# An attention and feed-forward block: turning tiles in 32 by 32 blocks on VectorE, and the mixing in two halves

## What is computed

```
qkv = x @ qkv_w + qkv_b;  16 heads of 16;  local attention over the 128 newest tokens -> local
latent part: 64 pooled tokens, 4 heads; softmax; remote = lat_out @ rout_w + rout_b
gate  = sigmoid(local @ gl_w + remote_h @ gr_w)            # one value per token and head
mixed = gate * local + (1 - gate) * remote_h
x1 = layernorm(x + mixed @ out_w + out_b)
h  = gelu(ternary_linear(x1, w_up));  y = layernorm(x1 + ternary_linear(h, w_down))
```

## Time and profile before

| | |
|---|---|
| median of three runs | 1155.28 us (1149.62 to 1156.93) |
| the profiled execution | 1154.15 us, of which the span of its instructions is 1152.4 us |
| PE busy | 88% of the span |
| DVE / POOL / ACT busy | 78% / 61% / 59% |
| mean granted PE clock | 0.965 |
| one sequence in the steady part | 66 us (first exponentials at 483.05 and 549.12 us) |

### The profile page before, as it was taken

How to read it: one execution, slowest core, us unless ns; L and a number is a source line. 1 busy time by engine, 2 the same in 40 slices (tenths; PEclk the granted TensorE clock), 3 DMA queues, 4 the chain that set the end, 5 groups by cost and what they waited for, 6 DMA issues and landing times.

```text
span 1152.4 us, 37627 instructions
## 1 busy us (share of the span) xinstructions
PE 1019.2 (88%) x15616; PEld 642.4 (56%) x15616; DVE 902.5 (78%) x2119; ACT 682.4 (59%) x1076; POOL 698.0 (61%) x874
## 2 busy tenths in 40 slices
PE   5878999999999999999999999999999999986855
PEld 2445565655556565655656565565656555564533
DVE  6688888887887988787888888788788878875445
ACT  2425666656666665666666565666666566664523
POOL 7216675656667576566757565566756565673744
PEclk9889999999999999999999999999999999996877
DMA  7740604325060423416061331616042250600000
GB/s 219 204 125 14 193 21 120 87 77 148 32 193 23 145 61 104 121 42 182 24 167 56 113 94 59 166 33 187 28 131 77 85 139 33 174 23 20 2 19 18
DMA packets 46662, 108.18 MB, mean 94 GB/s; under 512 B 7542, under 2 KB 26486, under 8 KB 43382
## 3 DMA queue, kind: packets, MB, share of 16 engines
q1 hardware_dynamic: 46348, 105.78, 31.9%
q10 hardware_dynamic: 144, 0.00, 0.0%
HBM read 71.58 MB, written 34.08 MB: 92 GB/s over the span
## 4 chain that ended last, share of the span: by engine, by line
PE 44%; DVE 28%; ACT 16%; issue 5%; POOL 3%; DMA 2%; SPq 1%; DVEq 0%; POOLq 0%; ACTq 0%
PE oacc L1459 8%; PE work L1537 7%; PE oacc L1480 6%; PE work L1398 5%; PE scores L1439 4%; ACT Pt L792 4%; PE work L1469 3%; DVE Pt L974 3%; DVE nmax L1048 3%; DVE x L1111 2%; DVE rem L1115 2%; PE scores L1377 2%; ACT hbuf L828 2%; PE work L1403 2%; DVE oT L1176 2%
## 5 line engine op out<-in xcount | busy, mean ns | idle before, releaser
L792 ACT ACTIVATE Pt<-scores 128x1024 f32<-128x1024 f32 (+1 forms) x256 | 228.6, 915 | 104.5 <-PE oacc L1459 63.8
L1048 DVE TENSOR_REDUCE nmax<-work 128x3 f32<-128x480 f32 x352 | 218.1, 637 | 25.2 <-PE work L1403 20.0
L656 POOL TENSOR_TENSOR h_lo<-hbuf,h_hi 128x512 f16<-128x512 f32 x128 | 148.2, 1158 | 130.7 <-DVE h_hi L1170 130.7
L628 POOL TENSOR_SCALAR_AFFINE_SELECT Pt<-Pt 128x512 f32<-128x512 f32 x256 | 166.8, 652 | 91.2 <-ACT Pt L792 90.0
L615 POOL TENSOR_TENSOR parts<-Pt,parts 128x512 bf16<-128x512 f32 x64 | 72.9, 1157 | 138.2 <-ACT parts L728 138.2
L1459 PE MATMUL oacc<-Pt,Vp 128*32 128x256 f32 (+1 forms) x2048 | 150.2, 360 | 5.8 <-DVE ytok L1192 2.7
L1398 PE MATMUL work<-Ks,Qs 98*32 98x160 bf16 x4096 | 139.8, 235 | 11.4 <-DVE nmax L1048 7.4
L1439 PE MATMUL scores<-Qs,Ks 100*32 100x160 bf16 (+4 forms) x4096 | 114.8, 230 | 23.5 <-ACT Pt L792 15.9
L1480 PE MATMUL oacc<-wdn_t,h_hi 128*128 128x256 f16 x512 | 118.2, 273 | 5.6 <-POOL h_lo L656 5.6
L632 POOL TENSOR_SCALAR_AFFINE_SELECT Pt<-Pt 128x512 f32<-128x512 f32 x192 | 122.0, 635 | 0.0
L1297 PE MATMUL scores<-xT,wqk 128*128 128x512 f32 x256 | 114.9, 602 | 6.1 <-DMA xT<-x_t 6.1
(11 more groups left out here) (158 smaller groups left out, 1952.9 us busy)
## 6 DMA issues: line engine op xcount, KB each, us to landing
parts_scratch<-parts SPq DMA_DIRECT2D x96, 256.0 KB, 4.5
Qs<-parts_scratch SPq DMA_DIRECT2D x96, 256.0 KB, 4.7
Ks<-parts_scratch SPq DMA_DIRECT2D x96, 256.0 KB, 4.9
xT<-x_t SPq DMA_DIRECT2D x16, 512.0 KB, 6.6
xres<-x SPq DMA_DIRECT2D x16, 512.0 KB, 7.2
y<-ytok SPq DMA_DIRECT2D x16, 512.0 KB, 3.4
nat<-up_t SPq DMA_DIRECT2D x1, 1024.0 KB, 9.6
nat<-down_t SPq DMA_DIRECT2D x1, 1024.0 KB, 11.8
```

Of the source, the lines that this page charges most:

```text
L628: ins = pool.affine_select(out=pt[:, :, 0:P], in_=pt[:, :, 0:P], compare_op=ALU.is_gt, fill=0.0, base=0, pattern=[[0, 4], [1, P]], channel ...
L656: pool.tensor_tensor(h_lo[:, t % NR, :], hbuf[:, t % 2, :], h_hi[:, t % NR, :], ALU.subtract).then_inc(h_lo_ready, 1)
L792: nc.scalar.activation(Pt[:, u % NPT, :, 0:w], scores[:, slot, :, :].rearrange("p k (h q) -> p (k h) q", h=2)[:, :, 0:w], ACT.Exp, scale=S ...
L1048: nc.vector.tensor_reduce(nmax[:, :, :].rearrange("p b h -> p (b h)")[:, first:first + n], work[:, slot, 0:n * BAND].rearrange("p (h c) -> ...
```

## The change

The output of a head group is turned by DVE straight from `oacc`, in blocks of 32 by 32 (`nc.vector.transpose`), so that tokens mod 32 lie on the partitions of each quadrant, and heads are spread over the four quadrants. The `O` transposes on PE and ACT's copy to `oT` go. The remote part is made transposed by PE (weights stationary, 256 tokens moving: four products, and a fifth for the gate's column in `REMOTE + 1`), ACT adds the bias into `remT` and `remgT` in five passes of 128x256, and DVE turns them into the same form. The gate's ops work on it; the exponential becomes a tanh. The mixing is done for 256 tokens at a time: two products and a sum of 128x512, and a block transpose straight into `mixT`, which `OUT` of that half reads; `MIX_T`, its transposes and ACT's copies go. The two `OUT` steps move up beside `QK + 3`. The maxima are turned by DVE once per sequence (`split_maxima`, at u = 16) and go into `Qs` by 16 small DMAs with no stop in DRAM; their place in SP's queue is now before the store. The reciprocals after the powers go (power of -0.5). ACT does the four last normalising passes, in `GATE` and at `QK + 2` of the next sequence. `pooled` is made one sequence earlier, after `UP + 6`. Weights' columns are put in the order of the quadrants on the host.

The core of the diff, in the order of the file:

```diff
-    ("F", GATE), ("P", QK), ("P", QK + 1), ("P", QK + 2), ("P", QK + 3), ("F", MIX_T),
-    ("P", LAT_RQ), ("F", OUT), ("P", LAT_RKV), ("F", OUT + 1), ("P", VALUES), ("P", LAT_SCORES), ("F", NORM),
+    ("F", GATE), ("P", QK), ("P", QK + 1), ("P", QK + 2), ("F", OUT), ("P", QK + 3),
+    ("F", OUT + 1), ("P", LAT_RQ), ("P", LAT_RKV), ("P", VALUES), ("P", LAT_SCORES), ("F", NORM),
...
+POOL_AT = ("F", UP + 6)
+NORMALISE_AT = {("F", GATE): (0, 1), ("P", QK + 2): (2, 3)}
...
-                for t in range(2):
-                    slot, k = work_use(s, "T", t)
...
+                wait_alone(sp, nmax_split, count(s, 1, 0))
+                for j in range(2):
+                    row = Qs[s.par][MAXR + j:MAXR + j + 1, :, :].rearrange("a h n -> a (h n)").rearrange(
+                        "a (k r w) -> a k r w", k=2, w=P)
+                    for g in range(NG):
+                        quadrant = slice(g * GT, (g + 1) * GT)
+                        for k in range(2):
+                            sp.dma_start(row[:, k, :, quadrant], nmax_pair[quadrant, j, k * GT:(k + 1) * GT]
+                                         ).then_inc(nmax_in[s.par], 16)
...
             def body(s):
                 later = s.second_next()
-                if later.exists:
-                    load_x(later)
+                if s.third_next().exists:
+                    load_x(s.third_next())
                 load_xres(s)
+                if not s.last:
+                    move_max(s.next())
                 if not s.first:
                     store_before(s)
-                if not s.last:
-                    move_max(s.next())
                 if later.exists:
...
+                if k == REMOTE:
+
+                    if not s.first:
+                        act.wait_ge(rem_turned, count(s, 2, -1))
+                    for i in range(2):
+                        bank, n = p_use(s, R_REM + i)
+                        act.wait_ge(p_full[bank], n + 1)
+                        for t in range(KT):
+                            ins = nc.scalar.activation(remT[:, t, i * HALF:(i + 1) * HALF],
+                                                       p_bank(bank)[:, t * HALF:(t + 1) * HALF], ACT.Identity,
+                                                       bias=brem[:, t:t + 1])
+                        ins.then_inc(p_taken[bank], 1)
...
-            def copy_o(s, hg):
-
...
+            def normalise_before(s, b):
+
+                if b == 0:
+                    act.wait_ge(fin_ready, count(s, 1, -1))
+                nc.scalar.activation(y2[:, b, :], y2[:, b, :], ACT.Identity, scale=fin[:, 0, b:b + 1],
+                                     bias=fin[:, 1, b:b + 1]).then_inc(y_ready, 1)
...
-                    nc.scalar.activation(gate[:, 1, :, :], gate[:, 0, :, :], ACT.Exp, scale=-1.0
+                    nc.scalar.activation(gate[:, 1, :, :, :], gate[:, 0, :, :, :], ACT.Tanh, scale=0.5
                                          ).then_inc(gate_e, 1)
-                if k == MIX_T:
-                    for t in range(KT):
-                        act.wait_ge(mix_T, count(s, KT, t))
-                        nc.scalar.activation(mixT[:, t, :], oacc[:, t, :], ACT.Copy).then_inc(mixT_in, 1)
...
+                if k == REMOTE:
+                    dve.wait_ge(rem_copied, count(s, 2, 0))
+                    for t in range(KT):
+                        ins = nc.vector.transpose(rem[:, s.par, t, :, :].rearrange("p b d -> p (b d)"), remT[:, t, :])
+                    ins.then_inc(rem_turned, 1)
+                if k == REMOTE + 1:
+                    dve.wait_ge(rem_copied, count(s, 2, 1))
+                    nc.vector.transpose(remg[:, s.par, :, :].rearrange("p b d -> p (b d)"), remgT[:, :]
+                                        ).then_inc(rem_turned, 1)
...
+            def split_maxima(s):
+
+                for v in (NM - 2, NM - 1):
+                    slot, k = work_use(s, "A", v)
+                    dve.wait_ge(w_taken[slot], k + 1)
+                if not s.first:
+                    dve.wait_ge(nmax_in[1 - s.par], (s.half + s.par) * 16 * 4 * NG)
+                nc.vector.transpose(nmaxT[:, :], nmax[:, :]).then_inc(nmax_vec, 1)
+                dve.wait_ge(nmax_vec, count(s, 2, 0))
+                nc.vector.tensor_copy(nmax_pair[:, 0, :], nmaxT[:, :]).then_inc(nmax_vec, 1)
+                dve.wait_ge(nmax_vec, count(s, 2, 1))
+                nc.vector.tensor_tensor(nmax_pair[:, 1, :], nmaxT[:, :], nmax_pair[:, 0, :], ALU.subtract
+                                        ).then_inc(nmax_split, 1)
 
             def take_o(s, hg):
 
-                slot, k = work_use(s, "O", hg)
-                dve.wait_ge(w_full[slot], k + 1)
...
+                dve.wait_ge(pv_done, count(s, NU, NB * hg + NB - 1))
+                nc.vector.transpose(o_q[:, hg // 2, :, hg % 2, :],
+                                    oacc[:, hg % 2, :].rearrange("p (b d) -> p b d", d=GT)).then_inc(o_taken, 1)
...
-                    z, e, ng, r, a = (gate[:, j, :, :] for j in range(5))
-                    done(nc.vector.tensor_tensor(e, o_tok[:, :, :, VN], dead[:, :, :], ALU.add))
-                    done(nc.vector.reciprocal(r, e))
-                    done(nc.vector.tensor_tensor(a, o_tok[:, :, :, HD], r, ALU.mult))
-                    nc.vector.tensor_tensor(z, a, rem[:, s.par, :, D:RW], ALU.add).then_inc(gate_z, 1)
+                    dve.wait_ge(o_taken, count(s, HG, HG - 1))
+                    z, e, ng, r, a, half_r = (gate[:, j, :, :, :].rearrange("p t b m -> p (t b m)")
+                                              for j in range(6))
+                    of_heads = o_q[:, :, :, :, :].rearrange("p t b m d -> p (t b m) d")
+                    done(nc.vector.tensor_tensor(a, of_heads[:, :, VN],
+                                                 dead[:, :, :, :].rearrange("p t b m -> p (t b m)"), ALU.add))
+                    done(nc.vector.reciprocal(r, a))
+                    done(nc.vector.tensor_tensor(a, of_heads[:, :, HD], r, ALU.mult))
+                    dve.wait_ge(rem_turned, count(s, 2, 1))
+                    for t in range(KT):
+                        of_t = [gate[:, j, t, :, :].rearrange("p (i b) m -> p i b m", i=2) for j in (0, 4)]
+                        remote = remg[:, s.par, :, :].rearrange("p b (i r) -> p i b r", i=2)
+                        ins = nc.vector.tensor_tensor(of_t[0], of_t[1], remote[:, :, :, 2 * t:2 * t + 2], ALU.add)
+                    ins.then_inc(gate_z, 1)
+                    mark(nc.vector.tensor_scalar(half_r, r, 0.5, None, ALU.mult))
                     dve.wait_ge(gate_e, count(s, 1, 0))
-                    done(nc.vector.tensor_scalar(z, e, 1.0, None, ALU.add))
-                    done(nc.vector.reciprocal(e, z))
...
+                    mark(nc.vector.tensor_scalar(ng, e, -0.5, 0.5, ALU.mult, ALU.add))
+                    sync()
+                    done(nc.vector.scalar_tensor_tensor(out=a, in0=e, scalar=1.0, in1=half_r,
+                                                        op0=ALU.add, op1=ALU.mult))
+
+                    def of_half(t4, i):
+                        return t4[:, :, i * G32 // 2:(i + 1) * G32 // 2]
+
+                    for i in range(2):
+                        mark(nc.vector.tensor_tensor(
+                            mixed[:, i, :, :].rearrange("p t (k d) -> p t k d", d=HD),
+                            of_half(o_q, i)[:, :, :, :, 0:HD].rearrange("p t b m d -> p t (b m) d"),
+                            of_half(gate[:, 4, :, :, :], i).rearrange("p t b m -> p t (b m)").unsqueeze(3
+                                ).to_broadcast([P, KT, G32, HD]), ALU.mult))
+                        half_rem = of_half(rem[:, s.par, :, :, :], i).rearrange("p t b (m d) -> p t (b m) d", m=2)
+                        mark(nc.vector.tensor_tensor(
+                            half_rem, half_rem, of_half(gate[:, 2, :, :, :], i).rearrange(
+                                "p t b m -> p t (b m)").unsqueeze(3).to_broadcast([P, KT, G32, HD]), ALU.mult))
+                        sync()
+                        done(nc.vector.tensor_tensor(mixed[:, i, :, :], mixed[:, i, :, :],
+                                                     of_half(rem[:, s.par, :, :, :], i).rearrange(
+                                                         "p t b d -> p t (b d)"), ALU.add))
+                        nc.vector.transpose(mixT[:, i, :, :].rearrange("p t n -> p (t n)"),
+                                            mixed[:, i, :, :].rearrange("p t n -> p (t n)")).then_inc(mixT_in, 1)
...
-                if NB + 2 <= u < 2 * NB + 2:
-                    b = u - NB - 2
...
+                    dve.wait_ge(y2_vec, count(s, NB + 1, -1))
+                    nc.vector.tensor_scalar(fin[:, 2, :], mv[:, :, 1], EPS, None, ALU.add).then_inc(var2_ready, 1)
+                if u == NB + 2:
+                    dve.wait_ge(rstd2_ready, count(s, 1, -1))
```

(23 more changed lines are left out.)

333 lines of the change are left out of this document (141 added, 192 removed).

## The result

The changed kernel takes 1172.7 us (median of 4 runs, 1170.2 to 1175.8), the kernel before 1155.0 beside it: a ratio of 1.016, 95% interval 1.012 to 1.021. That is slower, outside the forecast's range of 1105 to 1167, and on the other side of zero. The profiled execution has a span of 1171.6 us where that of before has 1152.4.

The account below looks back on a forecast made before the run. No single engine was taken to set the period. 14 sequences at -0.8 (-1.3 - 1.2 + 1.7) gave -11.2, the last two -11.1, prologue and end +0.9: -21.4 from 1154.15, 1132.8, so about 1134 us, range 1105 to 1167.

Parts of the forecast that it names:

- The block transpose: DVE's turn of 512 elements per partition, taken as 0.69 us, with 0.43 and 1.25 as ends.
- The slow turns: Rival: each 512-element DVE turn takes 1.25 us, +3.0 us per sequence, kernel at 1179; chance 0.09.
- table load: Gate: the tanh shares a table set with the exponential, so no load is added.
- First half, -1.3: First half of each sequence: turns leaving PE save 1.3 us, range 0.8 to 2.3.
- The sign: First half: POOL's gaps would be closed if the forecast was right.
- Gate, -1.2: Gate of each sequence: 1.2 us shorter, range 0.5 to 2.1, with ACT's `lat_bd` the next late thing.
- Tail, +1.7: Tail of the UP steps, each sequence: 1.7 us longer, range +0.8 to +2.9, DVE without a gap.
- cover ends here: Tail: DVE's 4.4 us of idle no longer hide the new work, which comes in series with the last sum.
- the rival's 1169: Clock rival: PE's tail wait of about 2 us lowers the steady clock, 2.5 us per sequence, kernel 1169; chance 0.13.
- Prologue, +0.9 with the end: Prologue loses a turn but gains a waiting pooling, +0.5; with the kernel's end, +0.9 us.
- The last two sequences, -11.1: Last two sequences: gates 4.8 and 4.0 us shorter, first halves 1.3 and 1.0, together -11.1 us.
- the paragraph on queues: SP's queue: 16 maxima DMAs ahead of store and `restack` hold nothing unless an issue costs over 0.45 us.

Follow-up runs that it names:

- f3_tail: Changed kernel with the pooling moved from behind UP+6 to behind UP+4 and VectorE's remote turns behind the last sum of squares: 1155.1 us.
- g2_adds: On top of f3_tail, GpSimd adds the residual's bias only after both mixing halves are turned; the output's first half waits for two of four additions: 1146.7 us.
- h3_all_qk: On top of h1_all, the fourth QK product goes ahead of the first output product on all engines: 1138.7 us.
- f1_fill: Changed kernel with harmless TensorE products added where it waits, in the gate and at the tail: 1167.5 us.
- g1_copies: On top of f3_tail, ScalarE's remote copies go behind the square of UP+7 and VectorE's turns ahead of the output's step: 1171.4 us.
- i1_all_remg: On top of h1_all, only the last of ScalarE's remote copies moves from ahead of the last gelu to behind its square: 1129.4 us.
- g3_ends: On top of f3_tail, prologue magnitude passes go behind the remote copies; ScalarE issues 8 of 16 maxima transfers for the first and last sequence: 1147.2 us.
- h1_all: Changed kernel with the edits of f3_tail, g2_adds and g3_ends together: 1135.8 us.

## Why the prediction was wrong

**The block transpose** was right: 1.31 us for two of 128x512 back to back, 0.69 forecast for one. The slow turns didn't happen, and no table load was added.

**First half, -1.3: right in size.** From the output's step to the next last weighted sum it was 22.23 us before, 21.32 after, and 20.89 in f3_tail, where the clock mostly holds at its start: -0.9 as built, -1.3 without the low clock. The mechanism is shown in part. The sign was that GpSimd's gaps are closed, and they are not: those that begin over 4 us behind the first scores add up to 2.4 us before, 1.7 after and 1.65 in f3_tail (means of ten sequences). Of the 1.0 us that I took from them 0.7 to 0.8 came; where the rest comes from is open.

**Gate, -1.2: failed.** Counted to the first gelu the gate became 0.66 us longer. The order of the forecast held, `lat_bd` included, for which VectorE waits 0.45 us in the changed kernel. What I had at nothing is what VectorE's small operations cost beside GpSimd's large ones. The changed kernel, VectorE's timeline and then GpSimd's:

```profile
528.74 1.09 DVE L1194 TENSOR_TENSOR rs<-mv,eps 128x6 f32<-128x6 f32 x1
...
532.81 0.39 DVE L1030 SCALAR_TENSOR_TENSOR rv_bd<-scores,brv 64x32 f32<-64x32 f32 x2 [0.45 <-ACT lat_bd L761]
...
533.97 0.93 DVE L1204 SCALAR_TENSOR_TENSOR nbias<-mv,rs 128x2 f32<-128x2 f32 x1
...
527.53 3.40 POOL L636 TENSOR_TENSOR parts<-Pt,parts 128x512 bf16<-128x512 f32 x3 [9.27 <-ACT parts L749]
...
532.44 1.33 POOL L663 TENSOR_TENSOR rs<-rs,power 128x6 f32<-128x6 f32 x1 [0.22 <-DVE rs L1194]
533.74 1.15 POOL L636 TENSOR_TENSOR parts<-Pt,parts 128x512 bf16<-128x512 f32 x1
```

The variance of `OUT + 1` was forecast at +15.3 after the last weighted sum and came at +16.4, because the operation at the gate's head took 0.71 for 0.26 and the last one of `OUT` 1.09 for 0.17. Behind it the last step of the first scale took 0.93 for 0.16. Together that is 2.1 us, in 12 of the 13 sequences 2 to 14; in the other almost only the second is held. In the kernel before, the additions ended at 506.17 and VectorE's gate began at 506.18, so its trace showed no hold there: the change pulled VectorE's gate under them. g2_adds removes the first and the third and most of the second, and 0.95 us of the gate with them, up to 0.3 of it by the clock. Then GpSimd's queue is the bound: the second power, 1.33 us on six elements for 1.02 on four, runs straight behind the first, VectorE waits for it, and the next operation is held for 0.96 us. (In the changed kernel itself the second power waits for VectorE.) h3_all_qk shows only that `lat_bd` is not the bound there. With the additions out of the way the gate is 0.3 us shorter than before, not 1.2. My estimate is that without the last hold it would be near the forecast, 0.3 + 0.96; that was not run.

**Tail, +1.7: the term was too large, and what follows it was missing.** From the first gelu to the last sum it is 18.16 us for 16.97, so +1.2 (from the start of UP+5 9.31 for 8.10; the sequence shown above has 9.5). I forecast that VectorE would have no gap and that "cover ends here", and priced nothing behind the sum. But with TensorE's waits of 0.62 and 0.70 us there the clock fell, which I had as a rival with its own condition and a price of 2.5 us per sequence: the condition was met, and the price was about a third of that (0.6 to the first scores and 0.3 in the first half, by the means of f1_fill). That the rival's 1169 lies near the result is luck: its mechanism explains 5 us of 17.7. And ScalarE's five copies (the expectation of g1_copies counts six) delay the chain of gelus by 0.56 us (15.50 for 14.94 between the first and the last), which I had at +4.75 against +4.0 inside the sum and let end in VectorE's queue; in f3_tail, where that queue is gone, it is still there, and i1_all_remg takes 0.50 of it out.

**Prologue, +0.9 with the end: failed.** The first gate was 5.7 us later. VectorE took that product from PSUM itself before; now it waits for ScalarE's copies, which stand behind 3.9 us of magnitude passes, and all maxima are queued behind it. The changed kernel, ScalarE's timeline:

```profile
46.61 1.94 ACT L891 ACTIVATE hbuf<-nat 128x2048 bf16<-128x2048 f32 x1
...
48.50 1.93 ACT L891 ACTIVATE xnT<-nat 128x2048 f16<-128x2048 f32 x1
...
50.40 1.58 ACT L786 ACTIVATE remT<-scores,brem 128x256 f32<-128x256 f32 x4
```

and VectorE's:

```profile
52.06 1.30 DVE L1079 STREAM_TRANSPOSE rem<-remT 128x512 f32<-128x512 f32 x2 [3.56 <-ACTq L791]
```

I followed the steps that moved and not the queue that the new step was put into. g3_ends moves both this and half of the transfers' issue, and 2.8 of the 5.7 us are left; which has what part, and what the rest is, stays open.

**The last two sequences, -11.1: half failed.** From the last gate to the end it was -3.6 for the -4.8 forecast. The one before lost 2.6 instead of winning some 4 to 5: "16 issues in 4.3 us" took 10.2, and the scores waited 11.82 us. The condition in the paragraph on queues, "nothing held unless an issue costs over 0.45 us", was the right one with the wrong side taken; in the steady part the late restack had no cost that any run shows.

**Sum.** Against the changed kernel: tail 17.6, additions 8.4, ends 7.9, the last copy 6.5 us. With the first three taken out the change gives 1135.8, with all four 1129.4. By the means of the ten sequences a period changed as follows: the gate +0.55 us for the forecast's -1.2, from the first gelu to the last sum +1.2 for +1.7, from there to the first scores +0.7 for nothing, the first half -1.0 for -1.3; together +1.5 for -0.8. The gate, with its holds at nothing, is the largest miss. That h1_all lies within 2 us of 1134 is partly luck: its gate gives 0.3 and not 1.2, and its tail costs 0.6 and not 1.7.

## What to carry to other kernels

When a step moves to another engine or another place, write down that engine's whole queue there, and what each later entry in it releases: the turns, the pooling and the copies were short operations standing ahead of ones that others waited for. Where VectorE and GpSimd both work, also draw their instructions over one another: a small operation of VectorE took up to the whole length of the GpSimd instruction beside it (1.11 us for 0.15 beside one of 1.17), so GpSimd's free work belongs beside VectorE's PSUM operations, and what the move puts beside the next small operation has to be drawn again. And a wait of TensorE that ends on time for its own chain can be free, as `lat_bd`'s is in h1_all; the same wait in the changed kernel, 2.27 us, went with the low clock and cost 0.3, and one at a boundary that the next stage starts from costs its length and, through the clock, some more.
